# Two of eight tiles sorted by place and fetched by GpSimd, with a payload copy moved behind the mask copy

## What is computed

```python
qkv = fuse(dwconvs(conv1x1(x_sorted)))          # five maps of 32 channels
q1, k1, q2, k2, v = split(qkv, 5)
idx = argsort(v.reshape(b, c, 3136))            # every row of v is sorted
vs  = take_along_axis(v, idx)
out1 = attn(gat(q1), gat(k1), vs, boxed=True)   # gat: q, k in the order of v
out2 = attn(gat(q2), gat(k2), vs, boxed=False)
out1, out2 = undo(out1, idx), undo(out2, idx)   # back to pixel order
out = conv1x1(out1 * out2, w_proj)
```

## Time and profile before

| what | us |
| --- | --- |
| median of three runs | 17449.1 |
| the profiled execution's own time | 17449.24 |
| its span, first to last instruction | 17447.5 |
| VectorE busy | 15663.8 (90%) |
| ScalarE busy | 7787.0 (45%) |
| GpSimd busy | 3410.5 (20%) |
| mean granted TensorE clock | 0.689 of full speed |

### The profile page before, as it was taken

The page is one execution under the profiler, slowest core; times in us unless marked ns, Lnnn a source line. Parts: engine busy times, 40 slices in busy tenths (PEclk is TensorE's granted clock), DMA queues, the critical chain, the costliest instruction groups (busy, mean ns, idle before and its releaser), DMA issues.

```text
span 17447.5 us, 110014 instructions
## 1 busy us (share of the span) xinstructions
PE 6697.1 (38%) x40644; PEld 2793.7 (16%) x40644; DVE 15663.8 (90%) x10298; ACT 7787.0 (45%) x5610; POOL 3410.5 (20%) x3271
## 2 busy tenths in 40 slices
PE   6888856554500255136226324612732112210010
PEld 4444421111100111012012111101211010100000
DVE  6999988899999899899889989988998987888978
ACT  0000013344444444544444454454444447878854
POOL 0000000004777777777500000000000000000000
PEclk9999978777755577568558657856865555655555
DMA  0000012201110011011001000000000001121232
GB/s 18 16 21 25 13 40 71 74 31 39 26 14 13 12 35 24 12 29 30 12 9 38 14 9 30 22 9 20 27 14 9 31 9 55 50 84 54 69 74 64
DMA packets 404197, 542.35 MB, mean 31 GB/s; under 512 B 157165, under 2 KB 363213, under 8 KB 392965
## 3 DMA queue, kind: packets, MB, share of 16 engines
q1 hardware_dynamic: 297892, 517.35, 10.3%
q0 software_dynamic: 105760, 17.87, 1.9%
HBM read 314.45 MB, written 220.38 MB: 31 GB/s over the span
## 4 chain that ended last, share of the span: by engine, by line
DVE 55%; ACT 10%; issue 8%; PE 6%; DMA 1%; SPq 1%; DVEq 0%; ACTq 0%; POOLq 0%
DVE arena L1100 19%; DVE arena L1093 19%; DVE arena L1713 3%; DVE psum L1069 3%; DVE arena L1077 3%; PE psum L1497 3%; ACT arena L1043 2%; PE psum L957 2%; ACT arena L1660 2%; DVE arena L1711 2%; ACT masks L997 1%; DVE arena L1084 1%; ACT arena L1372 1%; ACT arena L1355 1%; DVE arena L1566 1%
## 5 line engine op out<-in xcount | busy, mean ns | idle before, releaser
L1043 ACT ACTIVATE arena<-arena 128x2048 f32<-128x2048 f32 (+22 forms) x1274 | 2682.6, 2125 | 4749.3 <-DVE arena L1100 4748.7
L957 PE MATMUL psum<-arena,wt 128*32 128x448 f32 x31360 | 3309.5, 585 | 2221.9 <-DMA arena<-xpad 1212.9
L1093 DVE COPY_PREDICATED arena<-psum,arena 128x2048 f32<-128x2048 uint32 (+22 forms) x1274 | 3450.3, 2724 | 510.9 <-ACT masks L997 509.9
L1226 POOL DMA_INDIRECT arena<-payd,arena x3136 | 3331.5, 1062 | 1060.4 <-issue 936.6
L1100 DVE COPY_PREDICATED arena<-psum,arena 128x2048 f32<-128x2048 uint32 (+22 forms) x1274 | 3424.8, 2703 | 36.8
L957 PEld LDWEIGHTS psum<-arena,wt 128*32 128x32 f32 x31360 | 1026.8, 117 | 4506.6 <-issue 2673.6
L1450 PE MATMUL psum<-ident,arena 128*112 128x128 f32 x896 | 203.8, 396 | 3478.4 <-ACT arena L1372 2348.2
L1713 DVE COPY_PREDICATED arena<-arena 128x2048 f32<-128x2048 uint8 (+28 forms) x364 | 972.3, 2687 | 278.1 <-ACT arena L1670 277.9
L736 PE MATMUL psum<-arena 128*128 128x392 f32 x3072 | 1053.9, 496 | 32.1 <-DVE arena L638 32.0
L1033 ACT ACTIVATE arena<-arena 128x64 f32<-128x64 f32 (+34 forms) x798 | 789.3, 1025 | 522.3 <-DVE arena L1084 444.8
L1660 ACT ACTIVATE arena<-masks 128x4704 uint8<-128x4704 uint8 (+20 forms) x156 | 966.5, 6195 | 89.1 <-DMA masks<-row_masks 89.1
(11 more groups left out here) (142 smaller groups left out, 8920.2 us busy)
## 6 DMA issues: line engine op xcount, KB each, us to landing
arena<-xpad SPq DMA_DIRECT2D x896, 108.5 KB
arena<-payd,arena POOLq DMA_INDIRECT x3136
xpad<-arena SPq DMA_DIRECT2D x8, 1924.0 KB, 7.0
arena<-in_x SPq DMA_DIRECT2D x8, 1568.0 KB, 10.3
x3d<-arena SPq DMA_DIRECT2D x8, 1568.0 KB, 5.2
prodd<-arena SPq DMA_DIRECT2D x8, 1568.0 KB, 5.2
arena<-prodd SPq DMA_DIRECT2D x8, 1568.0 KB, 13.8
arena<-x3d SPq DMA_DIRECT2D x8, 1568.0 KB, 10.1
```

The source lines that it names most:

```text
L957: last = nc.tensor.matmul(psum[C * b:C * b + C, n % C_BANKS, 0:CROWS * W], wt[:, g, C * w:C * w + C], cx[i % 2][b][:, y0:y0 + CROWS, x0:x0 ...
L1043: last = nc.scalar.activation(packed_view(ptmp, here, piece, NP), pair_views(pay[b], piece, NP)[0], ACT.Copy)
L1093: last = nc.vector.copy_predicated(lo, wide_mask(q, piece, at), hi)
L1226: nc.gpsimd.indirect_dma_start(gout[k][:, NP * j:NP * j + NP], None, payd, bass.IndirectOffsetOnAxis(ap=gix[k][:, j:j + 1], axis=0)).then_ ...
```

## The change

Tile 6 is sorted by place too, so there are two short sorts (tiles 6 and 7), two sets of DRAM buffers, and two gathers by GpSimd, one after the other. Long sorts are left for tiles 0 to 5. SyncE, not GpSimd, stores places and values, at the start of the next round (`p_store`). In the long sort `keep_pay(s, 1)` now stands behind `mask_copy(s)`. The last long sort (tile 5) has five slots a stage, and beside it attention 4, the load of tile 6 and attention 6; it has no convolution. The first undoing round has five slots too, and beside it attention 5, the load of tile 7 and attention 7. The fifth slot of VectorE is behind the stage's last move. The cut diff (changes of mere names, as `vrow[0]` to `vrow[x]`, are left out):

```diff
-        def d_sync(sp, t, beside):
+        def d_sync(sp, t, beside, slots=SLOTS):
...
-                    for _ in range(SLOTS):
+                    for _ in range(slots):
                         next(beside, None)
...
             def keep_pay(q, k):
                 if q:
                     act.wait_ge(d_hi[k], q)
-                if q == LAST_LEVEL and k == 0:
-                    act.wait_ge(d_hi[1], q)
+                if q == LAST_LEVEL:
+                    act.wait_ge(d_hi[1 - k], q)
...
             keep_v(0)
             keep_pay(0, 0)
-            keep_pay(0, 1)
             for s in range(SR):
                 mask_copy(act, s)
+                keep_pay(s, 1)
                 if s + 1 < SR:
                     keep_v(s + 1)
                     keep_pay(s + 1, 0)
-                    keep_pay(s + 1, 1)
-                for _ in range(SLOTS):
+                for _ in range(slots):
                     next(beside, None)
...
                 upper(s, 1)
+                for _ in range(4, slots):
+                    next(beside, None)
...
-        def s_sync(sp, t, beside):
-            sp.dma_start(payd.rearrange("(p n) w -> p (n w)", p=P), pay[0]).then_inc(s_pay, 16)
+        def p_store(sp, x):
+
+            sp.dma_start(posd[x], upos[x]).then_inc(p_st[x], 16)
+            sp.dma_start(vsd[x], vrow[x]).then_inc(p_st[x], 16)
+
+        def s_sync(sp, t, x, beside):
+            if x:
+                p_store(sp, x - 1)
+            sp.dma_start(payd[x].rearrange("(p n) w -> p (n w)", p=P), pay[x]).then_inc(s_pay, 16)
             d_sync(sp, t, beside)
             sp.wait_ge(s_pay, 16)
...
-        def p_pool(pool):
-
-            pool.dma_start(posd, upos).then_inc(p_st, 16)
-            pool.dma_start(vsd, vrow[0]).then_inc(p_st, 16)
-            pool.wait_ge(p_st, 16 * 2)
+        def p_pool(pool, x):
+
+            pool.wait_ge(p_st[x], 16 * 2)
...
-        def h_load_sync(sp):
-            sp.wait_ge(p_done, 1)
-            sp.dma_start(pay[0], payq).then_inc(h_ld, 16)
-            sp.dma_start(vrow[0], vsd).then_inc(h_ld, 16)
+        def h_load_sync(sp, x):
+            sp.wait_ge(p_done, x + 1)
+            sp.dma_start(pay[x], payq[x]).then_inc(h_ld, 16)
+            sp.dma_start(vrow[x], vsd[x]).then_inc(h_ld, 16)
...
         def u_first_scalar(act):
...
-                yield from pace.to(12 + 12 * w)
+                yield from pace.to(14 + 12 * w)
...
-        def u_sync(sp, r, beside):
+        def u_sync(sp, r, beside, slots=SLOTS, late=60):
...
-                for _ in range(SLOTS):
+                for _ in range(slots):
                     next(beside, None)
-                if i == 60:
+                if i == late:
...
         @block.sync
...
-                b_sync(sp, u, c_sync(sp, T - 1, C_FIRST[n], 1) if n else iter(()), U_ORDER[n + 1] if n + 1 < U else None)
+                b_sync(sp, u, c_sync(sp, T - 2, C_FIRST[n], 1) if n else iter(()), U_ORDER[n + 1] if n + 1 < U else None)
...
-            s_sync(sp, T - 1, c_sync(sp, 0, CHUNKS, SLOTS))
-            close_round(sp, d_sems + c_sems + [s_pos, s_pay])
+            for x in range(NX):
+                s_sync(sp, T - 2 + x, x, c_sync(sp, (T - 1, 0)[x], CHUNKS, SLOTS))
+                close_round(sp, d_sems + c_sems + [s_pos, s_pay], LONG if x else ALL)
+            p_store(sp, NX - 1)
...
-            d_sync(sp, T - 3, chain(e_sync(sp, T - 4), c_sync(sp, T - 2, CHUNKS, SLOTS)))
-            close_round(sp, d_sems + e_sems + c_sems, LONG)
-            d_sync(sp, T - 2, chain(padded(e_sync(sp, T - 3), E_SLOTS), padded(h_load_sync(sp), 8),
-                                    padded(e_sync(sp, T - 1, hs), E_SLOTS), u_first_sync(sp)))
+            d_sync(sp, T - 3, chain(padded(e_sync(sp, T - 4), E_SLOTS), padded(h_load_sync(sp, 0), 8),
+                                    padded(e_sync(sp, T - 2, hs), E_SLOTS), u_first_sync(sp)), 5)
             close_round(sp, d_sems + e_sems + h_sems + u_first_sems, LONG)
+            u_sync(sp, 0, chain(padded(e_sync(sp, T - 3), E_SLOTS), padded(h_load_sync(sp, 1), 8),
+                                e_sync(sp, T - 1, hs)), 5, 68)
+            close_round(sp, e_sems + h_sems + u_sems + [*p_st, p_done], LONG)
             sp.sem_inc(go["pool"], 1)
-            u_sync(sp, 0, e_sync(sp, T - 2))
-            close_round(sp, e_sems + u_sems)
             u_sync(sp, 1, iter(()))
...
         @block.gpsimd
...
             s_pool(pool)
             end_round(pool, "pool")
-            p_pool(pool)
+            s_pool(pool)
+            for x in range(NX):
+                p_pool(pool, x)
             pool.wait_ge(go["pool"], 1)
             pool.sem_clear(go["pool"])
-            end_round(pool, "pool")
             end_round(pool, "pool")
```

More of the change, by code:

```diff
@@ L195, in program @@
         rd = nc.dram_tensor("rd", (B * C, N), f32).ap()
[L196 to L199 removed]
+        NX = 2
+        payd = [nc.dram_tensor(f"payd{x}", (P * N, NP), f32).ap() for x in range(NX)]
+        posd = [nc.dram_tensor(f"posd{x}", (P, N), mybir.dt.uint32).ap() for x in range(NX)]
+        vsd = [nc.dram_tensor(f"vsd{x}", (P, N), f32).ap() for x in range(NX)]
+        payq = [nc.dram_tensor(f"payq{x}", (P, N * NP), f32).ap() for x in range(NX)]
         row_masks = nc.dram_tensor("row_masks", (T, P, ROW_PAIRS), u8).ap()
@@ L1025, in d_sync, with d_scalar @@
                 sp.wait_ge(d_mst[i], 16 * count[i])
-        def d_scalar(act, b, beside):
+        def d_scalar(act, b, beside, slots=SLOTS):
             def keep_v(q):
@@ L1059, in d_scalar, with d_vector @@
                 pass
-        def d_vector(dve, b, beside):
+        def d_vector(dve, b, beside, slots=SLOTS):
             def compare(q):
@@ L1119, in program @@
         s_pos, s_pay = sem("s_pos"), sem("s_pay")
-        p_st, p_ix, p_gat, p_out, p_done = (sem("p_st"), [sem(f"p_ix{k}") for k in range(2)], [sem(f"p_gat{k}") for k in range(2)],
+        p_st, p_ix, p_gat, p_out, p_done = ([sem(f"p_st{x}") for x in range(NX)], [sem(f"p_ix{k}") for k in range(2)], [sem(f"p_gat{k}") for k in range(2)],
                                             [sem(f"p_out{k}") for k in range(2)], sem("p_done"))
@@ L1124, in program @@
         stmp = ptmp[:, N:N + TMP]
-        upos = pay[0][:, 0:N].bitcast(mybir.dt.uint32)
+        upos = [pay[x][:, 0:N].bitcast(mybir.dt.uint32) for x in range(NX)]
         st = [WS_AT + 8448]
@@ L1234, in p_pool @@
             pool.dma_reset()
-            for x in (*p_ix, *p_gat, *p_out):
-                pool.sem_clear(x)
+            for done in (*p_ix, *p_gat, *p_out):
+                pool.sem_clear(done)
             pool.sem_inc(p_done, 1)
@@ L1245, in program @@
         h_ld = sem("h_ld")
-        h_sems = [*hs.values(), h_ld, p_st, p_done]
+        h_sems = [*hs.values(), h_ld]
         st = [WS_AT]
@@ L1651, in u_sync, with u_scalar @@
                     sp.wait_ge(u_ld[w], 16)
-        def u_scalar(act, r, beside):
+        def u_scalar(act, r, beside, slots=SLOTS):
             def braid(i):
@@ L1701, in u_scalar, with u_vector @@
                                      ACT.Copy).then_inc(u_ev, 1)
-        def u_vector(dve, beside):
+        def u_vector(dve, beside, slots=SLOTS):
             def move(i, k, side):
@@ L1947, in _ @@
                 end_round(dve, "dve")
-            s_vector(dve)
-            end_round(dve, "dve")
-            d_vector(dve, 1, iter(()))
+            for x in range(NX):
+                s_vector(dve, x)
+                end_round(dve, "dve")
+            d_vector(dve, 0, iter(()))
             end_round(dve, "dve")
             with dve.Fori(0, (T - 4) // 2):
-                for k in (0, 1):
-                    d_vector(dve, k, e_vector(dve, 1 - k))
+                for k in range(2):
+                    d_vector(dve, 1 - k, e_vector(dve, k))
                     end_round(dve, "dve")
-            d_vector(dve, 0, e_vector(dve, 1))
+            d_vector(dve, 1, chain(padded(e_vector(dve, 0), E_SLOTS + 8), e_vector(dve, 0, hs)), 5)
             end_round(dve, "dve")
-            d_vector(dve, 1, chain(padded(e_vector(dve, 0), E_SLOTS + 8), e_vector(dve, 0, hs)))
-            end_round(dve, "dve")
-            u_vector(dve, e_vector(dve, 1))
+            u_vector(dve, chain(padded(e_vector(dve, 1), E_SLOTS + 8), e_vector(dve, 1, hs)), 5)
             end_round(dve, "dve")
@@ L1986, in _ @@
                 end_round(pe, "pe")
-            for _ in range(2):
+            for _ in range(3):
                 c_tensor(pe, CHUNKS)
@@ L1990, in _ @@
             with pe.Fori(0, (T - 4) // 2):
-                for k in (0, 1):
-                    e_tensor(pe, 1 - k)
+                for k in range(2):
+                    e_tensor(pe, k)
                     c_tensor(pe, CHUNKS)
                     end_round(pe, "pe")
-            e_tensor(pe, 1)
-            c_tensor(pe, CHUNKS)
-            end_round(pe, "pe")
-            e_tensor(pe, 0)
-            e_tensor(pe, 0, hs)
-            end_round(pe, "pe")
```

(6 more changed lines are left out.)

46 lines of the change are left out of this document (21 added, 25 removed).

## The result

The changed kernel takes 16527.7 us (median of four, 16526.6 to 16530.4), the kernel before 17449.9 in the same set: a ratio of 0.9471, interval 0.9455 to 0.9488, 922 us less. The forecast was 16602, 847 less, with a range of 16450 to 16800.

What follows compares the result with a forecast made beforehand. VectorE was taken to bound the long sort, except where ScalarE's attention work stands between lot 1's copy and the mask's. From 17449: +773 - 7418 - 1622 + 5768 + 1525 + 130 - 1.5 gave 16602 us, range 16450 to 16800.

Steps and rivals of the forecast that it cites:

- The second short sort: Extra short sort with the gather beside it: adds 773 us, the gather costing VectorE nothing; a late landing could cost 20.
- The gathers' end: Second gather by GpSimd ends by 13060, before SyncE asks at 14050 in the undoing, so it costs nothing.
- Rule and trace of the shared port: By the rule GpSimd might stand for 393 us of a short sort's tensor_tensor, ending about 13450; the sum stays.
- The order: Long sort, mask copied ahead of lot 1's copy: 42 of 74 us of mask waits go per attention.
- the ten long waits: Ten mask waits of 3.8 us or more per one-attention round, 54.7 us together, lose 2.2 each, not 3.2.
- the last long sort: Tile 5's long sort, five slots and two attentions: 1622 us becomes 1525, bounds 1440 and 1622.
- The tail and the fifth slot: End of the last long sort: with 390 slots a tail of about 38 us goes; five-piece crowding adds 20.
- The undoing: First undoing round with two attentions: 1196 + 90 for the second attention + 40 = 1326 us, bounds 1226 and 1420.
- the crowding: First undoing round: 40 us added for VectorE's waits for ScalarE's copies with five pieces and SyncE one stage ahead.
- The sum: Whole kernel: short sort, long sorts and undoing together change by -846 us, giving 16602 us.
- more goes than I say: Rival: both waits vanish nearly wholly and the undoing's second attention costs only 33 us: 16365 us; chance 0.10.
- The late gather: Rival: SyncE waits for the second gather in the undoing, kernel slower; 1.9 us a fetch gives 17700; chance 0.02.

Runs made afterwards that it cites:

- two pieces behind the mask: Changed kernel; in the long sort ScalarE does two pieces of side work right behind the mask copy and lot 1's copy, the rest before the next mask; 24725.2 us.
- the later store: Changed kernel; first undoing round: SyncE stores attention products ten slots later, second attention begins 20 slots later, late loads start at stage 72; 24827.0 us.

## Why the prediction was right, point by point

**The second short sort** was to cost 773 and cost 779. Three of the 6 us are the cut of the earlier trace rows: the short sort of before is 776 us long. GpSimd did not hold VectorE up (busy 723.1 us there, 724.6 in the short sort without a gather); VectorE's waits for ScalarE's mask copies rose from 30.2 to 35.8 us. The fetches aren't behind that, since the round takes 780 us without them too. The gathers' end was said to be 13060 and was 13127, and SyncE asked at 13994 (14050 said).

**Rule and trace of the shared port.** GpSimd did 483 fetches from 4131.7 to 4892 beside the short sort, one in 1.57 us, against one in 1.42 beside a long sort (1003 in 1427 us). The x502 and x1043 of the stretches count all of GpSimd's instructions, and so did the forecast's "1088 and 989 of them"; the fetches were 1046 and 949. By the Trainium skill's rule (SBUF — State Buffer, section "SBUF: two separate sides"), taken as a full block during the 393 us of tensor_tensor, an estimate is 367 us left, some 290 fetches of 1.25 us (0.94 and the 0.31 between two). For a single fetch the trace agrees with the rule; for the round it does not agree with that estimate. Of the 483 fetches 292 took 1 us or less. Of the 191 longer ones 190 began while a tensor_tensor ran, and they ended 0.82 us (median; eight tenths of them between 0.81 and 0.85) behind the end of that instruction. A few are held through more than one. The longest but one began in a compare (L1179) and ended at 4182.44, 0.77 us behind the end of the next tensor_tensor (L1185):

```profile
4176.86 2.46 DVE L1179 TENSOR_TENSOR psum<-arena 128x1176 f32<-128x1176 f32 x1
...
4177.40 5.04 POOL L1233 DMA_INDIRECT arena<-payd,arena  x1 [0.30 <-issue]
...
4179.19 2.48 DVE L1185 TENSOR_TENSOR arena<-arena 128x1176 f32<-128x1176 f32 x1
...
4181.70 2.42 DVE L1190 TENSOR_TENSOR arena<-arena 128x1176 f32<-128x1176 f32 x1
```

So a fetch that begins in a tensor_tensor stands until that instruction ends, and is mostly finished beside the one after it: these instructions slow the row of fetches and don't stop it. The 241 fetches that began beside a predicated copy took at most 0.99 us. VectorE's busy time shows no loss (723.1 us, and 727.0 without the fetches).

**The order.** The mechanism was right, and the size was too small: 42 us of 74 were to go, 50.2 went, and a round with one attention lost 56, 14 more than forecast. Eight of the 14 are the step that failed, the argument about the ten long waits: "a chain of work that goes on over three stages gains its earlier start once. I take 2.2 each". Of these 54.7 us and the small ones' 19.7 there are 23.8 left, about 3 us less for each long wait, as if they were independent. The kernel with two pieces behind the mask shows that no such chain was the limit: no mask wait is left in its rounds with one attention. Three more are the product's waits (12.8 to 9.9), and the last three neither; the round without attention gained 4.6 us (1366.0 to 1361.4), where the forecast had 1.5, and nothing for the rounds with one. In four rounds this was 57 us of the forecast's error. In the last long sort it was 34: mask waits of 62.2 where the sum had 80, the product's 23.9 where it had 36, and 4 by which 1521 had been rounded up. With the new order alone the mask waits of that round are 44.1 (137.1 before), so the order took 93 of them, where the sum had 84, and the fifth slot with the load added 18, where it had 27.

**The tail and the fifth slot.** Right: the tail went, and going back to four slots costs 39 us in that round, by the same terms.

**The undoing.** 1326 forecast, 1339 measured, but two terms were wrong and nearly cancelled; that it came so near is luck. "The first attention cost 1196 - 1106 = 90" took the end of the second undoing round 23 us too early, at 16820; it closes at 16842.7 and is 1129 us long, so the first attention cost 67. The second cost 143, not 90 + 40: by the forecast's own terms the crowding was 76 us and not 40. The named cause was there: SyncE's two waits and the shift of the second attention are 36 us of the 210 of both attentions by experiment, and how much of that the one attention of before paid already is not known. The rest is put down to crowding of ScalarE's queue and the product's waits (15.5 us in the earlier trace rows, 43.3 after) by subtraction only.

**The sum.** Off by +6 in the second short sort, -3 in the round without attention, -57, -34 and +13: -75, and the forecast was 74 us high. Of the rivals, "more goes than I say" had the direction. The late gather, the only one on the slower side, was 870 us off where these kernels ran at full speed; something of its kind, but another mechanism, is what the last section shows. Its price was reckoned wrong: at 1.9 us a fetch the gathers would end at 16041, 1990 us past 14050, which gives some 18590 us and not 17700.

## What to carry to other kernels

When an engine keeps copies for another and does work of a third kind beside, put what is needed first ahead of what merely can be done first, and put the side work behind it: one moved copy was worth 337 us here, and splitting the side work around it some 143 more by the rounds, with no instruction saved. A queue that only issues transfers (SyncE) is an engine too: what waits in it, or is big and stands ahead of small urgent loads, reaches the busiest engine through ScalarE (36 us of a round for both, with the second attention shifted). Before moving more work to GpSimd's indirect DMAs, time it in several sets: their cost was nothing in the two sets in which they were left out, and in another the rounds beside them took thousands of us more.

## What the runs showed of the hardware that was not expected

In one of the four sets the kernel before took 21564 us (21535 to 21570) in place of 17450, and the kernels with two gathers 24725 to 24831 (e.g. the later store: ratio 1.1515, interval 1.1496 to 1.1535). Seven runs of the one and four of each of the others agree within 0.2%, so it is steady there. Each chip was in one set only, so whether it goes with the chip or with the time of the set is not shown. The loss stands in the rounds beside the fetches alone: in the four kernels of that set the second short sort took 4991 to 4994 us (779 elsewhere) and the long sort behind it 5462 to 5481 (1361), together 8314 to 8335 more; the first short sort and all rounds from 14600 on are as elsewhere. The kernel before lost 4114 us, about one such round.

Four stretches of the kernel with the later store (columns as above). The first two lie during the first gather, the third behind its last fetch and still in the second short sort, the fourth behind the second gather:

```profile
7000.00:7300.00 300.00, 105.58 (x131) 15.69 (x130) 11.29 (x5) 5.32 (x4) 208.03 (x223) 0.51 0.07 4
...
8300.00:8500.00 200.00, 69.61 (x77) 9.70 (x76) 7.51 (x5) 4.25 (x4) 140.58 (x150) 0.50 0.10 13
8530.00:8600.00 70.00, 70.00 (x740) 29.21 (x736) 56.50 (x41) 32.88 (x32) 0.00 (x0) 0.99 0.15 44
...
13600.00:13900.00 300.00, 145.72 (x1324) 44.09 (x1316) 295.91 (x173) 145.26 (x107) 0.00 (x0) 0.74 0.05 17
```

During the fetches VectorE is busy for 11 of 300 us, and TensorE has 131 matmul records instead of 1324. The first gather's last fetch begins at 8513.3; in the 100 us before there are 3 to 6 matmul records in each 10 us, and from 8530 on 99 to 108, of the same convolution. At the end of the second gather (13490.1) the rate is back within 30 us, and at the start of each (4132.9 and 9116.3) it falls to 4 or 5 in 10 us within some 70 us. GpSimd is not slow, its fetches have the usual length:

```profile
L1233 POOL DMA_INDIRECT arena<-payd,arena x6272: 938/942/2322, 4132.9 to 13490.1; - x196
```

The timeline shows what TensorE does:

```profile
7002.94 0.94 POOL L1233 DMA_INDIRECT arena<-payd,arena  x1 [0.46 <-issue]
7003.42 0.13 PEld L958 LDWEIGHTS psum<-arena,wt 128*32 128x32 f32 x1 [2.67 <-issue]
7004.34 0.94 POOL L1233 DMA_INDIRECT arena<-payd,arena  x1 [0.46 <-issue]
7004.82 0.91 PE L958 MATMUL psum<-arena,wt 128*32 128x448 f32 x1 [1.89 <-issue]
...
7016.02 0.91 PE L958 MATMUL psum<-arena,wt 128*32 128x448 f32 x1 [1.88 <-issue]
7016.08 0.94 POOL L1233 DMA_INDIRECT arena<-payd,arena  x1 [0.31 <-issue]
7017.33 0.94 POOL L1233 DMA_INDIRECT arena<-payd,arena  x1 [0.30 <-issue]
...
7018.58 0.94 POOL L1233 DMA_INDIRECT arena<-payd,arena  x1 [0.30 <-issue]
7018.82 0.91 PE L958 MATMUL psum<-arena,wt 128*32 128x448 f32 x1 [1.89 <-issue]
```

TensorE's weight loads and matmuls alternate, one of them every 1.40 us, so a matmul of 0.91 us every 2.80, and each waits for nothing that the profile can name ("issue"). The fetches, too, are 1.40 us apart in most of the stretch; where they are 1.25 apart (7016.08 to 7018.58), TensorE keeps its 2.80, so it isn't one instruction per fetch. The convolution's results then reach ScalarE some 300 us apart, ScalarE's mask copies stand behind them in its queue, and so does VectorE. VectorE's and ScalarE's own instructions are no longer than usual (the convolution's eviction takes 1.05 us here and 1.27 in the changed kernel). In the changed kernel's trace of the result, TensorE has 1252 matmul records in 300 us of the same round beside the same fetches (4400 to 4700). What differs between the sets was not found, and that the fetches are the cause there is read from this coincidence in time, at both ends of both gathers, and not shown by leaving them out. The changed kernel itself was not run in that set; its four variants were slower than the kernel before by 15%, which the forecast did not have.
